# Pixels in natural order on ScalarE; the selection reads columns eight apart, the tail interleaves four quadrants into every second PSUM column

## The chip, the core and the metric

One NeuronCore of a Trainium2 chip. The metric is the device time of one execution in microseconds (us); lower is better.

## What is computed

The input is x, 16 images of 512 channels and 64 x 64 pixels in fp32. Two residual layers follow each other. The change lies in the first one.

```python
def spatial_descriptor(x, k):
    b, c, h, w = x.shape
    p = k // 2
    xp = jnp.pad(x, ((0, 0), (0, 0), (p, p), (p, p)))
    corrs = [jnp.sum(x * jax.lax.dynamic_slice(xp, (0, 0, di, dj), (b, c, h, w)), axis=1) for di in range(k) for dj in range(k)]
    return jnp.stack(corrs, axis=1)
...
gs = spatial_descriptor(x, k)                                # k = 5: 25 correlations with the neighbours
norm = jnp.sqrt(jnp.sum(gs * gs, axis=1, keepdims=True) + EPS)
gs = gs / norm
feat = jnp.concatenate([x, gs], axis=1)
out = jnp.einsum('bchw,oc->bohw', feat, W) + bias[None, :, None, None]
return jax.nn.relu(out)
...
x = x + _L0_conv_ref(_gn(x), L0_conv_W, L0_conv_bias)        # first layer, _gn is a group norm of 32 groups
x = x + _L1_conv_ref(_gn(x), L1_conv_w1, L1_conv_b1, L1_conv_w2, L1_conv_b2)   # max pools, chosen by channel
```

## The kernel before, in words

The first layer runs over 16 images, each in 8 chunks (`c`) of 8 rows, 512 pixels; so there are 128 chunks. The 512 channels lie on the partitions in four blocks (`ct`, and `o` for the output's four blocks). Every engine has its own written-out program, and semaphores alone tie them together. In the turn of chunk c each does this:

- **ScalarE (ACT)** squares and roots the descriptor's norm (lines 535 and 537), empties the four conv banks of chunk c-1 with a ReLU into `relu` (`conv_out`, line 520), and normalises chunk c+3: for each channel block one activation writes the fp32 value `g32` (line 506) and one its fp16 rounding `gh` (line 508). Between the second and the third block it copies the transposed blocks out of PSUM (`after`, line 528).
- **VectorE (DVE)** masks the Gram products (line 726), makes the reciprocal and the descriptor `fn` (745, 749), adds the ReLU to the residual (738) and takes its statistics (740), and forms the fp16 remainder `gl` = `g32` - `gh` (`low_parts`, line 713), beside the next image's input statistics (663).
- **TensorE (PE)**, in this order: `picks` (line 1101), a Gram block (line 1056), `norm` (1123), a Gram block, `tail` of chunk c-1 (1134), two Gram blocks, the convolution's first output block (1079 to 1081), `turn_blocks` (1114), the other three output blocks.
- **GpSimd and the SyncE queue** split the descriptor into fp16 parts and regroup it with twelve small DMAs into `tpair`.

A Gram block multiplies the pixels of two rows with those of four rows. Its product has a pixel of the pair on each partition and on each column; `band` keeps the columns within two pixels, and `bq` holds the masked blocks. `picks` then takes the 25 correlations out with one-hot matrices, one for each of four quadrants `t` of 32 output partitions; a matmul has only 32 output columns of the array, and a group of four works side by side. `tail` adds the descriptor's part of the convolution to the four conv banks, with the regrouped descriptor as moving operand.

For the picks, the pixel's column w = 8 j + k is split by its class k = 2 t + q. Before the change, the pixels of a row pair are stored sorted by class: `turned` and `classed` are views by which ScalarE reads x in steps of eight fp32 (32 bytes) and writes `gh` and `g32` without gaps, and by which it reads a conv bank without gaps and writes `relu` in steps of eight. The Gram blocks, the picks and the conv banks then all have class order, and each pick reads runs of eight neighbouring columns.

Before the Gram block that opens turn c+1's work, TensorE waits on `s_gl` for VectorE's remainder of chunk c+2, which was normalised in the turn before.

Of the kernel before, what the change touches and what calls it, by code (L numbers as in the profile page):

```python
# [16 lines left out]
C, H, W = 512, 64, 64  # L17
# [4 lines left out]
CW = ROWS * W  # L22
NB = H // 2
PAIRS = ROWS // 2
# [10 lines left out]
RING = 4  # L35
# [5 lines left out]
REP = 3 * 32  # L41
QUADS = 4
# [2 lines left out]

def const_arrays():


    p = np.arange(P)
    k, r, j = p // 16, p // 8 % 2, p % 8  # L50
    w = 8 * j + k
    band = (np.abs(w[:, None] - w[None, :]) <= KS // 2).astype(np.float32)


    pick = np.zeros((P, 3, 2, QUADS, 32), np.float32)
    for role in range(3):
        for e in range(2):
            for t in range(QUADS):
                di = r + 2 * (1 - role) - e
                rho = (k - 2 * t + 2) % 8  # L60
                ok = (np.abs(di) <= KS // 2) & (rho < 6)
                pick[p[ok], role, e, t, (rho * KS + di + 2)[ok]] = 1.0
    ssum = (p[:, None] // 32 == p[None, :] // 32).astype(np.float32) * 2.0 ** -12
    gavg = (p[:, None] // CG == p[None, :] // CG).astype(np.float32) / CG
    ident = np.eye(P, dtype=np.float32)
    before = (p[:, None] < p[None, :]).astype(np.float32)
    ones = np.ones((P, P), np.float32)
    return np.concatenate([band, pick.reshape(P, -1), ssum, gavg, ident, before, ones], axis=1)
# [18 lines left out]
def build(nc, x, wt, wturn, bias, w1t, b1, w2t, b2, consts, out):  # L87
    fp32, fp16, i32 = mybir.dt.float32, mybir.dt.float16, mybir.dt.int32
    ALU, ACT, AX = mybir.AluOpType, mybir.ActivationFunctionType, mybir.AxisListType
# [17 lines left out]
    with ctx:  # L107
# [3 lines left out]
        def sb(name, shape, dt):  # L111
            return ctx.enter_context(nc.sbuf_tensor(name, shape, dt))
# [3 lines left out]
        o = 0  # L116
# [8 lines left out]
        bias_sb = sb("bias_sb", [P, CT], fp32)  # L125
# [10 lines left out]
        gbias = sb("gbias", [P, CT], fp32)  # L136
# [7 lines left out]
        def take(n):  # L144
            pos[0] += n
            assert pos[0] <= ARENA
            return arena[:, pos[0] - n:pos[0]]

        take(2 * CT * PIX)
        gh = take(CT * RING * CW // 2).bitcast(fp16).rearrange("p (t n) -> p t n", t=CT)  # L150
        gl = take(CT * RING * CW // 2).bitcast(fp16).rearrange("p (t n) -> p t n", t=CT)
        g32 = take(2 * CW).rearrange("p (s n) -> p s n", s=2)
# [7 lines left out]
        tpair = take(CW).bitcast(fp16).rearrange("p (s n) -> p s n", s=2)  # L160
        relu = take(2 * CW).rearrange("p (s n) -> p s n", s=2)
# [64 lines left out]
        psum = ctx.enter_context(nc.psum_tensor("psum", [P, 8, 512], fp32))  # L226
# [70 lines left out]
        def xs(ct, lo, n, par):  # L297

            return arena[:, bass.ds(par * (CT * PIX) + (ct * PIX + lo), n)]

        def turned(a):

            return a.rearrange("p (u r j k) -> p u k r j", r=2, j=8, k=8)

        def classed(a):

            return a.rearrange("p (u k r j) -> p u k r j", k=8, r=2, j=8)

        def gram_parts(t):


            parts, row = [], 2 * t
            while row < min(2 * t + 4, H):
                end = min(2 * t + 4, H, (row // (RING * ROWS) + 1) * RING * ROWS)
                parts.append(((row - 2 * t) * W, (row % (RING * ROWS)) * W, (end - row) * W))
                row = end
            return parts
# [170 lines left out]
        def _(act):  # L488
# [5 lines left out]
            def normalise(i, c, first=False, between=None):  # L494

                n0 = (i * CH + c) * CT
                act.wait_ge(s_newton, 3 * i + 3)
                if not first:

                    act.wait_ge(s_chunk_used, i * CH + c - RING + 1)  # L500
                for ct in range(CT):
                    if not (isinstance(n0, int) and n0 + ct < 2):
                        act.wait_ge(s_gl, n0 + ct - 1)
                    act.sem_inc(s_carry_a, 1)
                    piece = turned(xs(ct, c * CW, CW, i % 2))
                    act.activation(classed(g32[:, ct % 2, :]), piece, ACT.Identity, bias=gbias[:, ct:ct + 1],  # L506
                                   scale=grstd[:, ct:ct + 1])
                    act.activation(classed(gh[:, ct, (c % RING) * CW:(c % RING + 1) * CW]), piece, ACT.Identity,  # L508
                                   bias=gbias[:, ct:ct + 1], scale=grstd[:, ct:ct + 1]).then_inc(s_gh, 1)
                    if between and ct == 1:  # L510
                        between()

            def conv_out(chunk, o):
                n = chunk * CT + o
                act.wait_ge(s_conv, n + 1)
                if isinstance(n, int) and n < 2:
                    pass
                else:
                    act.wait_ge(s_added, n - 1)
                act.activation(turned(relu[:, o % 2, :]), classed(psum[:, o, :]), ACT.Relu, bias=bias_sb[:, o:o + 1],  # L520
                               scale=1.0 / (SC * SC)).then_inc(s_relu, 1)

            def after(i, c):
# [6 lines left out]
            def image(i, last):  # L530
                for c in range(CH):
                    n = i * CH + c
                    first = isinstance(n, int) and n == 0
                    act.wait_ge(s_pick, n + 1)
                    act.activation(sq, psum[:, BANK_A, 0:QW], ACT.Square).then_inc(s_sq, 1)
                    act.wait_ge(s_norm, n + 1)
                    act.activation(sq, psum[:, BANK_N, 0:QW], ACT.Sqrt, bias=epsd[:, :]).then_inc(s_root, 1)
                    if not first:
                        for o in range(CT):
                            conv_out(n - 1, o)  # L540
                    if c + 1 < CH:
                        turn = lambda: after(i, c + 1)
                    elif not last:
                        turn = lambda: after(i + 1, 0)
                    else:
                        turn = lambda: None
                    if c + 3 < CH:
                        normalise(i, c + 3, first=first, between=turn)
                    elif not last:
                        normalise(i + 1, c + 3 - CH, between=turn)  # L550
                    else:
                        turn()
                    if c == STATS_AT and not last:
                        group_root(i + 1)
# [3 lines left out]
            for c in range(3):  # L558
                normalise(0, c, first=True)
# [494 lines left out]
        def _(pe):  # L1054
# [30 lines left out]
            def picks(i, c):  # L1085

                pe.wait_ge(s_after, i * CH + c + 1)
                if not (isinstance(i, int) and i == 0 and c == 0):
                    pe.wait_ge(s_fn, i * CH + c)
                half = (c % 2) * PAIRS * P  # L1090
                for e in range(2):
                    for k, role in enumerate((BEFORE, AFTER, SAME)):

                        u0 = 1 if role == BEFORE and c == 0 else 0
                        u1 = PAIRS - 1 if role == AFTER and c == CH - 1 else PAIRS
                        src = bq[:, role, half:half + PAIRS * P]\
                            .rearrange("p (u t q r j) -> p t r q u j", t=QUADS, q=2, r=2, j=8)
                        for t in range(QUADS):
                            dst = psum[32 * t:32 * t + 32, BANK_A, 0:QW]\
                                .rearrange("p (q u r j) -> p r q u j", q=2, r=2, j=8)  # L1100
                            last = pe.matmul(dst[:, e, :, u0:u1, :], pick[:, role, e, t, :], src[:, t, e, :, u0:u1, :],
                                             start=(e == 0 and k == 0), stop=True, skip_group_check=True)
                last.then_inc(s_pick, 1)
# [21 lines left out]
            def tail(i, c):  # L1125


                half = c % 2
                pe.wait_ge(grouped[half], (i * (CH // 2) + c // 2 + 1) * GROUPED)
                src = tpair[0:REP, half, :].rearrange("p (t q u s) -> p q u t s", t=QUADS, q=2, u=PAIRS)  # L1130
                for o in range(CT):
                    dst = psum[:, o, :].rearrange("p (u t q s) -> p q u t s", u=PAIRS, t=QUADS, q=2)
                    for par in range(2):
                        last = pe.matmul(dst[:, par], wd[0:REP, par * C + o * P:par * C + (o + 1) * P],  # L1134
                                         src[:, par], start=False, stop=True, skip_group_check=True)
                    last.then_inc(s_conv, 1)
# [148 lines left out]
```

## Time and profile before

| | |
|---|---|
| median of 3 runs | 4606.43 us (4600.07 to 4608.84) |
| the profiled execution | 4614.89 us, span of its core 4613.1 us |
| PE busy | 3847.0 us, 83% |
| DVE busy | 3520.3 us, 76% |
| ACT busy | 2589.7 us, 56% |
| first layer's loop, 128 chunks | from 81.67 us to about 2,610 us |
| mean granted TensorE clock | 0.928 of full speed |

Busy shares are means over two very different stages: the loop over the chunks, in which PE is busy nearly all the time, and the second layer, in which DVE is. A change in the first layer has to be read from the loop's turns: what ends the last wait of the engine that all others follow.

### The profile page before, as it was taken

How to read it: one execution, taken by the hardware profiler on the slowest of the kernel's cores; microseconds unless marked ns; L12 is line 12 of the kernel's file. 1: busy time of each engine (PE TensorE's matmuls, PEld its weight loads, DVE VectorE, ACT ScalarE, POOL GpSimd, SP SyncE). 2: the span in 40 equal slices, each digit the busy share in tenths (PEclk: the TensorE clock that was granted, in tenths of full speed). 3: DMA queues.
4: the chain of work that ended last, by engine and by line, in shares of the span. 5: the costliest groups of instructions: out<-in, count | busy, mean ns of one | idle time of the engine just before them, and what ended most of it. 6: DMA issues, size and time to landing. Idle time of an engine off the chain costs nothing. (4 is left out here: it accounts for less than half of the span.)

```text
span 4613.1 us, 73329 instructions
## 1 busy us (share of the span) xinstructions
PE 3847.0 (83%) x23656; PEld 2135.8 (46%) x23657; DVE 3520.3 (76%) x4010; ACT 2589.7 (56%) x2830; POOL 637.1 (14%) x624
## 2 busy tenths in 40 slices
PE   3999999999999999999989767898888777777665
PEld 2655555555555555555556443343333333323222
DVE  5676667667666765766665576899999999999994
ACT  4777777777777777777777434443333233232322
POOL 0000000000000000000000012333232322222221
PEclk9999999999999999999999878898899888888887
DMA  4233322323333232333321246553333333323221
GB/s 167 97 116 116 109 103 100 134 98 116 116 116 111 99 120 97 116 116 116 115 98 61 61 129 217 180 182 154 146 147 134 132 143 125 134 107 123 111 119 48
DMA packets 174313, 556.98 MB, mean 121 GB/s; under 512 B 91248, under 2 KB 91248, under 8 KB 157552
## 3 DMA queue, kind: packets, MB, share of 16 engines
q1 hardware_dynamic: 152016, 283.62, 17.7%
q0 software_dynamic: 21920, 268.59, 15.1%
q8 instruction: 206, 3.38, 0.3%
q14 instruction: 171, 1.40, 0.1%
HBM read 277.23 MB, written 274.86 MB: 120 GB/s over the span
## 5 line engine op out<-in xcount | busy, mean ns | idle before, releaser
L931 DVE TENSOR_TENSOR arena<-arena 128x2048 f32<-128x2048 f32 (+4 forms) x730 | 1759.1, 2430 | 107.7 <-ACT arena L579 66.3
L1250 PE MATMUL psum<-arena 128*128 128x512 f32 x1072 | 615.0, 658 | 442.0 <-issue 399.0
L1056 PE MATMUL psum<-arena 128*128 128x256 f16 (+1 forms) x6344 | 744.2, 272 | 152.7 <-DVE arena L713 134.8
L579 ACT ACTIVATE arena<-arena 128x4096 f32<-128x4096 f32 x67 | 244.2, 3645 | 972.3 <-DVE arena L931 706.6
L1079 PE MATMUL psum<-arena 128*128 128x512 f16 x2048 | 782.3, 382 | 0.7 <-ACT arena L520 0.7
L1080 PE MATMUL psum<-arena 128*128 128x512 f16 x2048 | 782.3, 382 | 0.0
L1081 PE MATMUL psum<-arena 128*128 128x512 f16 x2048 | 782.1, 382 | 0.0
L520 ACT ACTIVATE arena<-psum,bias_sb 128x512 f32<-128x512 f32 x512 | 577.5, 1184 | 270.6 <-PE psum L1134 171.3
L1056 PEld LDWEIGHTS psum<-arena 128*128 128x128 f16 x6344 | 597.4, 99 | 241.5 <-issue 124.1
L713 DVE TENSOR_TENSOR arena<-arena 128x512 f16<-128x512 f32 x512 | 351.7, 687 | 432.0 <-ACT arena L508 431.9
L506 ACT ACTIVATE arena<-arena,gbias,grstd 128x512 f32 (+1 forms) x512 | 669.3, 1307 | 6.0 <-DVE arena L713 4.7
L508 ACT ACTIVATE arena<-arena,gbias,grstd 128x512 f16 (+1 forms) x512 | 668.6, 1306 | 0.0
L1254 PE MATMUL psum<-arena 128*128 128x512 f32 x1072 | 579.9, 624 | 0.0
L1250 PEld LDWEIGHTS psum<-arena 128*128 128x128 f32 x1072 | 217.7, 210 | 738.3 <-issue 674.3
L599 ACT ACTIVATE arena<-psum,arena 128x512 f32<-128x512 f32 x536 | 336.0, 689 | 321.8 <-PE psum L1254 321.4
L1252 PE MATMUL psum<-arena 128*128 128x512 f32 x896 | 500.7, 642 | 0.0
L738 DVE TENSOR_TENSOR arena<-arena 128x512 f32 (+1 forms) x512 | 349.4, 682 | 141.8 <-ACT arena L520 141.8
L740 DVE BATCH_NORM_STATS2 bny<-arena 128x6 f32 (+1 forms) x512 | 355.4, 694 | 98.2 <-DVE arena L738 96.0
L409 POOL CAST arena<-arena 128x128 f16<-128x128 f32 x128 | 37.4, 292 | 2510.4 <-DVE arena L749 2510.4
L1254 PEld LDWEIGHTS psum<-arena 128*128 128x128 f32 x1072 | 219.2, 204 | 290.1 <-issue 290.1
L663 DVE BATCH_NORM_STATS2 bnx<-arena 128x6 f32 (+1 forms) x512 | 326.2, 681 | 11.3 <-DMA arena<-in_x 11.2
L1081 PEld LDWEIGHTS psum<-arena 128*128 128x128 f16 x2048 | 201.6, 98 | 245.5 <-issue 7.0
(138 smaller groups left out, 2672.0 us busy)
## 6 DMA issues: line engine op xcount, KB each, us to landing
arena<-in_x SPq DMA_DIRECT2D x64, 2048.0 KB, 12.6
y_planes<-arena SPq DMA_DIRECT2D x64, 2048.0 KB, 7.9
arena<-arena SPq DMA_DIRECT2D x1536, 8.0 KB, 1.7
arena<-plane_records,arena POOLq DMA_INDIRECT x67, 3.0
arena<-y_planes,arena POOLq DMA_INDIRECT x67, 9.4
out<-arena POOLq DMA_INDIRECT x67, 8.7
arena<-in_wt SPq DMA_DIRECT2D x1, 1024.0 KB, 12.6
cst<-in_consts SPq DMA_DIRECT2D x1, 768.0 KB, 4.3
```

The lines of the kernel that those rows point to most:

```text
L506: act.activation(classed(g32[:, ct % 2, :]), piece, ACT.Identity, bias=gbias[:, ct:ct + 1], scale=grstd[:, ct:ct + 1])
L508: act.activation(classed(gh[:, ct, (c % RING) * CW:(c % RING + 1) * CW]), piece, ACT.Identity, bias=gbias[:, ct:ct + 1], scale=grstd[:, ct ...
L520: act.activation(turned(relu[:, o % 2, :]), classed(psum[:, o, :]), ACT.Relu, bias=bias_sb[:, o:o + 1], scale=1.0 / (SC * SC)).then_inc(s_ ...
L740: dve.bn_stats(bny[:, o, c, :], y).then_inc(s_y, 1)
L931: ins = dve.tensor_tensor(dst, a, b, ALU.max)
L1056: return pe.matmul(dst, w, m, start=(k == 0), stop=(k == nk - 1))
L1079: pe.matmul(dst, h, gh[:, ct, slot], start=(ct == 0), stop=False)
L1080: pe.matmul(dst, h, gl[:, ct, slot], start=False, stop=False)
L1081: last = pe.matmul(dst, l, gh[:, ct, slot], start=False, stop=(ct == CT - 1))
L1250: pe.matmul(dst, diag[:, s, 0, :], bufs[:, u, b * CW:(b + 1) * CW], start=True, stop=False)
L1252: pe.matmul(dst, diag[:, s, 1, :], small[:, s, b * ROWS:(b + 1) * ROWS, 1:W + 1], start=False, stop=False)
L1254: pe.matmul(dst, diag[:, s, 2, :], big[:, s, b * CW:(b + 1) * CW], start=False, stop=True)\
```

## The change

ScalarE reads and writes natural pixel order everywhere. The class order moves into TensorE's access patterns: the picks read columns eight apart, and the tail's output goes to every second column of the conv bank. The constants that hold the order of the pixels on the partitions (`band`, `pick`) follow. No instruction is added, removed or moved: on each engine the sequence of instructions is the same, and only the shapes of the patterns differ.

```diff
     p = np.arange(P)
-    k, r, j = p // 16, p // 8 % 2, p % 8
-    w = 8 * j + k
+    r, w = p // W, p % W
+    k = w % 8
     band = (np.abs(w[:, None] - w[None, :]) <= KS // 2).astype(np.float32)
...
-        def turned(a):
-            return a.rearrange("p (u r j k) -> p u k r j", r=2, j=8, k=8)
-        def classed(a):
-            return a.rearrange("p (u k r j) -> p u k r j", k=8, r=2, j=8)
...
-                    piece = turned(xs(ct, c * CW, CW, i % 2))
-                    act.activation(classed(g32[:, ct % 2, :]), piece, ACT.Identity, bias=gbias[:, ct:ct + 1],
+                    piece = xs(ct, c * CW, CW, i % 2)
+                    act.activation(g32[:, ct % 2, :], piece, ACT.Identity, bias=gbias[:, ct:ct + 1],
                                    scale=grstd[:, ct:ct + 1])
-                    act.activation(classed(gh[:, ct, (c % RING) * CW:(c % RING + 1) * CW]), piece, ACT.Identity,
+                    act.activation(gh[:, ct, (c % RING) * CW:(c % RING + 1) * CW], piece, ACT.Identity,
                                    bias=gbias[:, ct:ct + 1], scale=grstd[:, ct:ct + 1]).then_inc(s_gh, 1)
...
-                act.activation(turned(relu[:, o % 2, :]), classed(psum[:, o, :]), ACT.Relu, bias=bias_sb[:, o:o + 1],
+                act.activation(relu[:, o % 2, :], psum[:, o, :], ACT.Relu, bias=bias_sb[:, o:o + 1],
                                scale=1.0 / (SC * SC)).then_inc(s_relu, 1)
...
                         src = bq[:, role, half:half + PAIRS * P]\
-                            .rearrange("p (u t q r j) -> p t r q u j", t=QUADS, q=2, r=2, j=8)
+                            .rearrange("p (u r j t q) -> p t r q u j", t=QUADS, q=2, r=2, j=8)
...
-                src = tpair[0:REP, half, :].rearrange("p (t q u s) -> p q u t s", t=QUADS, q=2, u=PAIRS)
+                src = tpair[0:REP, half, :].rearrange("p (t q s) -> p q s t", t=QUADS, q=2)
                 for o in range(CT):
-                    dst = psum[:, o, :].rearrange("p (u t q s) -> p q u t s", u=PAIRS, t=QUADS, q=2)
+                    dst = psum[:, o, :].rearrange("p (s t q) -> p q s t", t=QUADS, q=2)
```

A pick's 64 columns were eight runs of eight fp32; they are now 64 fp32 each 32 bytes from the one before. A tail matmul's 256 fp16 were sixteen runs of sixteen neighbours, and its output went to runs of 16 columns; now each fp16 lies 256 bytes from the one before (after every fourth it jumps back by three such steps, less one element), and the output goes to 256 columns, every second one of the bank.

## Rows read from the trace of the kernel before

**Rows 1.** The page's header, busy times and slices.

```profile
span 4613.1 us, 73329 instructions
PE 3847.0 (83%) x23656; PEld 2135.8 (46%) x23657; DVE 3520.3 (76%) x4010; ACT 2589.7 (56%) x2830; POOL 637.1 (14%) x624
...
PE   3999999999999999999989767898888777777665
...
DVE  5676667667666765766665576899999999999994
ACT  4777777777777777777777434443333233232322
```

**Rows 2.** Waits from 500 to 2500 us: total us, times, longest.

```profile
ACT arena L520 <- PE psum L1134: 130.1, 99, 2.5
...
PE psum L1056 <- DVE arena L713: 99.1, 63, 1.9
...
PE psum L1142 <- ACT arena L528: 21.4, 12, 1.8
...
PE psum L1114 <- DVE arena L732: 4.8, 22, 0.3
```

**Rows 3.** PE in order of time: start, length, idle time before in brackets.

```profile
1555.20 0.38 PE L1081 MATMUL psum<-arena 128*128 128x512 f16 x1
1555.51 0.88 PE L1101 MATMUL psum<-arena,cst 128*32 128x64 f32 x48
1557.81 1.48 PE L1056 MATMUL psum<-arena 128*128 128x256 f16 x12 [1.42 <-DVE arena L713]
1559.12 0.39 PE L1123 MATMUL psum<-arena,cst 128*128 128x128 f32 x2
1559.35 1.47 PE L1056 MATMUL psum<-arena 128*128 128x256 f16 x12
1560.66 1.04 PE L1134 MATMUL psum<-arena 96*128 96x256 f16 x8
1561.53 2.81 PE L1056 MATMUL psum<-arena 128*128 128x256 f16 x36
```

**Rows 4.** ACT in order of time, the end of the same turn.

```profile
1554.43 1.31 ACT L506 ACTIVATE arena<-arena,gbias,grstd 128x512 f32 x1
1555.65 1.30 ACT L508 ACTIVATE arena<-arena,gbias,grstd 128x512 f16 x1
1556.86 0.25 ACT L535 ACTIVATE arena<-psum 128x128 f32<-128x128 f32 x1
```

**Rows 5.** Groups by form from 500 to 2500 us: count, busy us, mean ns.

```profile
L1123 PEld LDWEIGHTS psum<-arena,cst 128*128 128x128 f32 x200 | 31.8, 201 | 1.5
L506 ACT ACTIVATE arena<-arena,gbias,grstd 128x512 f32 x396 | 517.9, 1308 | 4.1 <-DVE arena L713 4.1
...
L520 ACT ACTIVATE arena<-psum,bias_sb 128x512 f32<-128x512 f32 x398 | 450.1, 1183 | 212.5 <-PE psum L1134 130.1 <-DVE arena L738 72.6
...
L528 ACT ACTIVATE arena<-psum 128x512 f32<-128x512 f32 x87 | 50.5, 580 | 0.0
...
L528 ACT ACTIVATE arena<-psum 128x384 f32<-128x384 f32 x13 | 6.1, 470 | 0.0
```

**Rows 6.** The same of the whole run: contiguous activation with a bias pointer.

```profile
L599 ACT ACTIVATE arena<-psum,arena 128x512 f32<-128x512 f32 x536 | 336.0, 689 | 321.8 <-PE psum L1254 321.4
```

**Rows 7.** Start of the run in order of time: first normalisation, first Gram block, later waits.

```profile
45.21 1.30 ACT L506 ACTIVATE arena<-arena,gbias,grstd 128x512 f32<-128x512 f32 x1 [1.33 <-DVE gbias L703]
...
55.66 4.15 PE L1056 MATMUL psum<-arena 128*128 128x256 f16 x24 [13.42 <-DVE arena L713]
...
74.05 0.69 DVE L713 TENSOR_TENSOR arena<-arena 128x512 f16<-128x512 f32 x1 [1.70 <-ACT arena L508]
...
75.22 4.58 PE L1056 MATMUL psum<-arena 128*128 128x256 f16 x24 [15.42 <-DVE arena L726]
```

**Rows 8.** DVE in order of time, one turn: first mask, first residual, last remainder.

```profile
1539.79 0.42 DVE L726 TENSOR_TENSOR arena<-psum,cst 128x256 f32<-128x256 f32 x1 [0.46 <-PE psum L1056]
...
1543.19 0.69 DVE L738 TENSOR_TENSOR arena<-arena 128x512 f32 x1 [1.07 <-ACT arena L520]
...
1549.85 0.67 DVE L713 TENSOR_TENSOR arena<-arena 128x512 f16<-128x512 f32 x1
...
1554.56 0.69 DVE L713 TENSOR_TENSOR arena<-arena 128x512 f16<-128x512 f32 x1 [0.99 <-ACT arena L508]
1555.17 1.28 DVE L663 BATCH_NORM_STATS2 bnx<-arena 128x6 f32 x2
1556.98 0.69 DVE L713 TENSOR_TENSOR arena<-arena 128x512 f16<-128x512 f32 x1 [0.53 <-ACT arena L508]
```

## The prediction

> **What bounds the kernel now.** I read the page's slices first. The run has two stages: up to slice 22 or 23 PE is in the nines while DVE and ACT have room, after that DVE is in the nines [rows 1]. The change touches nothing in the second stage, so the question is the length of a turn in the first. The norm's matmul shows two weight loads per turn, and 200 of them in 2,000 us give 100 turns of 20.0 us [rows 5].
>
> The waits come next. PE waits for DVE's remainder (L713) 99.1 us in those 100 turns, for ACT's copy (L528) 21.4 us, and 4.8 us for a mask [rows 2]: 125 us, 1.25 us a turn. Read against time, this is one chain. PE has finished its convolution and the picks by 1556.4 and starts the next Gram block at 1557.81 [rows 3]; the last remainder runs from 1556.98 [rows 8], and it waits for the last normalisation, which ACT starts at 1555.65 and ends at 1556.95 [rows 4]. So ACT, though it has idle time earlier in the turn (it waits 130.1 us for the tail's banks [rows 2]), delivers last and costs PE over a microsecond. The rest of the turn, 18.75 us, is PE's own work and sequencer pauses. The reader is to see that PE is nearly full and that ACT's lateness is the only large thing that a cheaper ACT can return.
>
> **What ACT gives back.** Twelve activations per turn lose their 32-byte steps. Now a normalisation takes 1308 ns and a ReLU 1183 [rows 5]. The nearest row without steps is the second stage's activation of 512 columns with a bias pointer, 689 ns [rows 6], so each gets about 0.6 us (normalisation) or 0.5 us (ReLU) shorter: 8 x 0.62 + 4 x 0.49 = 6.9 us per turn. ACT then has its normalisations done several microseconds before PE asks, and the waits for L713 and L528 go in full: -1.25 x 128 = -160 us. What is late next if nothing else changed is DVE: from its first mask (1539.79) to the start of the last remainder (1556.98) lie 17.2 us, with 0.99 and 0.53 of waits for ACT in it, and 1.07 for the first ReLU, which comes 0.5 earlier [rows 8]. Without these 2.0 us, and with the remainder itself (0.7 us) and the Gram block ahead of the first mask (1.3 us), the loop over DVE is some 17.2 us, under PE's 18.75. So PE's own work is the bound, and DVE's slack covers the gain.
>
> At the start PE waits 13.42 and then 15.42 us while ACT normalises three chunks alone; from 45.21 to the last remainder at 74.05 these are 24 activations of 1.2 us each from start to start [rows 7]. At 0.6 us each this is 24 x 0.6 = 14 us shorter. Sum of gains: 174 us.
>
> **What TensorE pays.** PE's work is on the path everywhere, so each nanosecond added to it counts 128 times.
>
> The tail: eight matmuls of 256 fp16 columns occupy 1561.53 - 1560.66 = 0.87 us, 109 ns each, 0.43 ns a column [rows 3]. The picks: 48 records in groups of four side by side are 12 steps in 0.88 us less the 0.22 that the last one takes to end, 55 ns for 64 columns, 0.87 ns a column [rows 3]. No row of PE shows a moving operand in which every column is a hop, nor an output to every second column. The bounds:
> - Below: no cost, as a run of 16 or of 8 neighbours reads at full rate.
> - Above, by the nearest row: ScalarE reads the same SBUF in the same 32-byte hops. Its normalisation costs (1308 - 689) / 512 = 1.2 ns a column more than the row without hops [rows 5, 6]; that row's slope is (580 - 470) / 128 = 0.86 ns a column [rows 5], so a hop costs about 2.0 ns. The ReLU, which only writes in hops, gives nearly the same.
> - Between: PE reads fp32 at 0.87 ns a word; if a hop takes two such slots, it is 1.74 ns.
>
> I take the middle of the last two, 1.87 ns a hopping column, because two independent streams on ScalarE (read and write) both show a price near 2 ns that belongs to the memory rather than to the engine, and because fp16 gives PE nothing to combine when neighbours are 256 bytes apart. Tail: 256 x 1.87 = 479 ns instead of 109, 8 x 0.370 = +2.96 us. Picks: 64 x 1.87 = 120 ns instead of 55 per step, 12 x 0.064 = +0.77 us. Together +3.73 us a turn, x 128 = +477 us.
>
> The Trainium skill (Advanced Engine Details and Errata, "Memory Cachelines") says that SBUF has 16-byte lines, that two hits on a line are needed to hide its latency, and that in PSUM any non-contiguous pattern significantly slows a matmul, pairs of neighbours being wanted. This speaks against both edited patterns; it gives no figure, and the trace agrees with its SBUF half on ScalarE (1308 against 689 ns), while no row shows the PSUM half.
>
> DVE's loop grows by less: the first ReLU comes after two tail matmuls, 0.74 us later, and 17.9 us stays under the turn of 22.5 that PE then has.
>
> **The sum.** On the profiled execution: 4614.9 - 174 + 477 = 4918. The profiled time stands 8.5 us over the median of the runs, so 4909 us. With 1.74 ns a hop the tail adds 2.69 and the picks 0.67 us, +430 us: 4862. With 2.0 ns, 3.22 + 0.87 = 4.09 us, +524 us: 4956. This likeliest case spans 4860 to 4960.
>
> **The rivals.**
> - The tail only doubles. If PE fetches each hop in one 0.83 ns slot of its word stream (or if only the output to every second column counts, two columns' time for one), a tail matmul takes 213 ns, +0.83 us a turn. With the picks dear (+0.77) this is 1.60 x 128 = +205 us: 4629. With the picks free it is +107 us: 4539. For it: PE's interface feeds fp16 at twice ScalarE's element rate, and the picks' four side-by-side streams show that it sustains more than one read at once [rows 3]. Against: ScalarE's price of a hop [rows 5].
> - TensorE doesn't mind hops at all, and the change does what ACT's rows promise: 4614.9 - 174 - 8.5 = 4432. For it: runs of 16 fp16 with jumps between already cost nothing, 109 ns for 256 columns like the Gram blocks (1.47 us for 12 and a tail end) [rows 3]. Against: ScalarE's reading, which is also free of any arithmetic reason to be slow.
> - Hops dearer than on ScalarE, as four pick streams start at nearly the same addresses and the tail's hops of 256 bytes may meet the same part of the memory: at 2.5 ns the tail adds 4.25, the picks 1.25 us, +704 us: 5137.
>
> The sign turns where PE's addition reaches 174 / 128 = 1.36 us a turn. With one price s for all 2048 tail and 768 pick columns, 2816 s = 0.87 + 0.67 + 1.36, s = 1.03 ns a column: under that the change is faster.
>
> **How the numbers follow.** Likeliest case 0.48; tail doubled with dear picks 0.15; tail doubled with free picks 0.13; free 0.11; dearer 0.13. The likeliest case's own range is 4860 to 4960; the range for 8 in 10 takes in both doubled cases below and a third of the dearer one above: 4530 to 5000. A measurement of this kernel tells 0.2% (9 us) from no change. Slower is the likeliest case, the dearer one and most of the first doubled case (0.11): 0.72; faster is free, doubled with free picks and a little of the other: 0.25; same 0.03.
>
> **What would show it.** Right: L506 and L508 near 690 ns, ReLU near 690; no wait of PE for L713 or L528 beyond a microsecond in all; tail matmuls starting over 400 ns apart, the picks' burst about 1.6 us, the turn 22.5 us, ACT idle waiting for the tail. Wrong on the price: tail matmuls 109 or 213 ns apart. Wrong on the gain: PE still waiting for L713 with DVE busy just before, or the Gram blocks and convolution slower though their patterns are as before.

## The result: 4.8% slower, and the profile after

The median of four runs is 4821.71 us (4818.33 to 4829.57) against 4603.25 us (4597.22 to 4608.84) before; the ratio is 1.0477, with a 95% interval of 1.0456 to 1.0498. The profiled execution has a span of 4823.3 us.

The page's header and busy times after. In kernels made from the change the line numbers are nine lower than before: L1056 is now L1047, L1101 L1092, L1134 L1125, L713 L704, L506 L497, L520 L511.

```profile
span 4823.3 us, 73329 instructions
PE 4235.3 (88%) x23656; PEld 2230.7 (46%) x23657; DVE 3528.9 (73%) x4010; ACT 1891.0 (39%) x2830; POOL 646.1 (13%) x624
```

ACT has lost 699 us of work and PE has gained 388; DVE's is the same [rows 1]. The next fence is the busy time by stretch, first of before, then of after, each from the first pick of the first turn to the first pick of the last, 127 turns. The columns are stretch and length, then PE, PEld, DVE, ACT and POOL busy with counts, granted clock, DMA share and GB/s.

```profile
81.70:2608.80 2527.10, 2335.72 (x20294) 1467.05 (x20294) 1670.14 (x3083) 1897.79 (x1900) 91.35 (x254) 0.99 0.30 105
```

```profile
69.80:2817.40 2747.60, 2722.82 (x20294) 1563.88 (x20294) 1678.52 (x3083) 1216.13 (x1900) 90.97 (x254) 0.99 0.27 97
```

The reader is to see three things. The loop starts 11.9 us earlier. A turn takes 2747.6 / 127 = 21.63 us where it took 19.90, 220.5 us more in the loop; 220.5 - 11.9 is 209 of the 210 us by which the two spans differ, so the second stage took no part. And PE's idle time is 24.8 us, 0.20 us a turn, where it was 191.4, 1.51 us a turn: the gain that was promised did come, and PE's own work grew by 387 us over it.

TensorE in order of time after, the counterpart of [rows 3]:

```profile
1602.74 1.49 PE L1092 MATMUL psum<-arena,cst 128*32 128x64 f32 x48
1604.16 1.48 PE L1047 MATMUL psum<-arena 128*128 128x256 f16 x12
1605.48 0.39 PE L1114 MATMUL psum<-arena,cst 128*128 128x128 f32 x2
1605.70 1.47 PE L1047 MATMUL psum<-arena 128*128 128x256 f16 x12
1607.02 3.64 PE L1125 MATMUL psum<-arena 96*128 96x256 f16 x8
1610.48 1.71 PE L1047 MATMUL psum<-arena 128*128 128x256 f16 x14
```

No bracket stands behind any row: nothing waits. Eight tail matmuls take 1610.48 - 1607.02 = 3.46 us, so they start 433 ns apart instead of 109; that is 1.7 ns a column. The picks are a burst of 1.49 us instead of 0.88. The Gram blocks, whose patterns the change leaves alone, keep their 1.48 us. The groups by form from 500 to 2500 us, and one row of the waits there:

```profile
L1125 PE MATMUL psum<-arena 96*128 96x256 f16 x736 | 335.3, 612 | 0.0
L497 ACT ACTIVATE arena<-arena,gbias,grstd 128x512 f32 x368 | 296.7, 806 | 129.3 <-DVE arena L704 129.3
...
L511 ACT ACTIVATE arena<-psum,bias_sb 128x512 f32<-128x512 f32 x368 | 252.9, 687 | 452.2 <-DVE arena L729 258.7 <-PE psum L1125 193.5
```

```profile
ACT arena L526 <- PE psum L1092: 357.1, 92, 7.0
```

A normalisation takes 806 ns (1308 before) and a ReLU 687 (1183) [rows 5]. PE's waits for DVE's remainder and for ACT's copy, 99.1 and 21.4 us in [rows 2], have left the list; now ACT waits for PE's picks.

### The profile page after: what moved, and what is told of

Its sections match the earlier page's. It is cut to its first block and busy times, and to the rows that moved or that the text cites. A ratio compares the mean times of both kernels' runs of the same rounds, so it can differ in the third digit from the quotient of the medians.

```text
span 4823.3 us, 73329 instructions
## 1 busy us (share of the span) xinstructions
PE 4235.3 (88%) x23656; PEld 2230.7 (46%) x23657; DVE 3528.9 (73%) x4010; ACT 1891.0 (39%) x2830; POOL 646.1 (13%) x624
## 5 line engine op out<-in xcount | busy, mean ns | idle before, releaser
L1047 PE MATMUL psum<-arena 128*128 128x256 f16 (+1 forms) x6344 | 750.3, 273 | 18.4 <-DVE arena L704 9.5
L1047 PEld LDWEIGHTS psum<-arena 128*128 128x128 f16 x6344 | 604.5, 100 | 195.8 <-issue 107.3
L717 DVE TENSOR_TENSOR arena<-psum,cst 128x256 f32<-128x256 f32 x448 | 187.7, 419 | 599.8 <-PE psum L1047 599.8
L511 ACT ACTIVATE arena<-psum,bias_sb 128x512 f32<-128x512 f32 x512 | 351.8, 687 | 632.6 <-DVE arena L729 353.9
L497 ACT ACTIVATE arena<-arena,gbias,grstd 128x512 f32 (+1 forms) x512 | 412.7, 806 | 166.7 <-DVE arena L704 165.4
L1125 PE MATMUL psum<-arena 96*128 96x256 f16 x1024 | 466.4, 612 | 0.0
L704 DVE TENSOR_TENSOR arena<-arena 128x512 f16<-128x512 f32 x512 | 343.4, 681 | 134.5 <-ACT arena L499 134.5
L499 ACT ACTIVATE arena<-arena,gbias,grstd 128x512 f16 (+1 forms) x512 | 409.7, 800 | 0.0
```

What stands on the lines that cost most here:

```text
L497: act.activation(g32[:, ct % 2, :], piece, ACT.Identity, bias=gbias[:, ct:ct + 1], scale=grstd[:, ct:ct + 1])
L499: act.activation(gh[:, ct, (c % RING) * CW:(c % RING + 1) * CW], piece, ACT.Identity, bias=gbias[:, ct:ct + 1], scale=grstd[:, ct:ct + 1]) ...
L1047: return pe.matmul(dst, w, m, start=(k == 0), stop=(k == nk - 1))
```

## The experiments

The theory after the result has two parts. The gain is the removal of PE's waits for ACT. The loss is PE's own, and within it a price of reading SBUF: a read brings up to 8 neighbouring bytes in a slot of about 1.7 ns, so a hop at every element wastes half of a slot with fp32 and three quarters with fp16. The main rival for the loss is the tail's output to single PSUM columns, which the change brought in at the same place; a rival for the whole is that ACT's and PE's parts interact. Time differences are against the change's 4822 us where nothing else is said. Where only one run was made, the time is that run's.

### ScalarE's half alone

```diff
-                            .rearrange("p (u r j t q) -> p t r q u j", t=QUADS, q=2, r=2, j=8)
+                            .rearrange("p (u t q r j) -> p t r q u j", t=QUADS, q=2, r=2, j=8)
...
-                src = tpair[0:REP, half, :].rearrange("p (t q s) -> p q s t", t=QUADS, q=2)
+                src = tpair[0:REP, half, :].rearrange("p (t q u s) -> p q u t s", t=QUADS, q=2, u=PAIRS)
...
-                    dst = psum[:, o, :].rearrange("p (s t q) -> p q s t", t=QUADS, q=2)
+                    dst = psum[:, o, :].rearrange("p (u t q s) -> p q u t s", u=PAIRS, t=QUADS, q=2)
```

> ScalarE in natural order as after the change, picks and tail with the access patterns of before, so the picks select and the tail places the wrong pixels; the amount of work is the same. It measures the gain alone. Theory (PE's waits for ScalarE go in full, PE's own work stays): 4603 - 1.25 x 128 - 12 at the start = 4431 us, a turn of 18.4 to 18.8 us, tail matmuls 109 ns apart. Rival (DVE's loop comes next and eats part of it): 4450 to 4550 us, with PE waiting for L713's successor and DVE busy just before.

Measured: 4407.5 us, ratio to before 0.9554 (0.9538 to 0.9570). The stretch of 127 turns, columns as above:

```profile
69.60:2410.40 2340.80, 2296.11 (x20294) 1463.03 (x20294) 1657.74 (x3083) 1202.19 (x1900) 94.44 (x254) 1.00 0.32 114
```

That is 18.43 us a turn, 1.47 less than before, and PE is idle for 0.35 us of it. ScalarE's half is worth 4.5%; its time is 24 us under the 4431 expected. Beside pauses of PE's sequencer, one wait of PE is left from 500 to 2300 us:

```profile
PE psum L1047 <- DVE arena L704: 10.2, 12, 0.9
```

DVE's loop thus takes back 0.1 us a turn. PE's idle time fell by 1.51 - 0.35 = 1.16 us a turn. The other 0.31 us is PE's busy time, which for the same matmuls is 2296.1 us where it was 2335.7. Part of that goes with the granted clock. Of the 85 slices of 20 us from 600 to 2300 us, 17 had a clock of 0.96 or less before, nearly all 0.91, and 4 have it here; 13 slices fewer at 20 x 0.09 = 1.8 us are an estimated 23 us.

### TensorE's half alone

The kernel before, with the constants, the picks and the tail of the change and ScalarE's `turned` and `classed` kept, so that its lines have the numbers of before.

> The other part of the change alone: picks and tail with the new patterns, ScalarE as before in its hops, so the picks and the tail take wrong pixels. The amount of work is the same. Theory (TensorE's work is the bound once it is longer, and ScalarE's lateness hides behind it): tail 435 ns, a turn of 21.7 to 21.9 us, 4822 + 12 for the slow start, 4834 to 4860 us; TensorE's waits for VectorE near zero. Rival (the tail lies on ScalarE's own loop, whose delay adds to it): 20.05 + 3.24 = 23.3 us a turn, 5020 us, with the waits of before.

Measured: 4862.84 us, ratio to before 1.0559 (1.0540 to 1.0579). The waits from 500 to 2500 us:

```profile
DVE arena L713 <- ACT arena L508: 288.4, 217, 2.2
...
PE psum L1142 <- ACT arena L528: 8.7, 12, 0.7
...
PE psum L1056 <- DVE arena L713: 5.1, 14, 0.4
```

DVE still waits for ACT, but PE hardly for DVE: 5.1 us where it was 99.1 [rows 2]. The halves don't add. ScalarE's is worth about 200 us alone and some 40 us beside TensorE's; TensorE's costs 255 us alone and 414 us beside ScalarE's (4822 - 4407.5). A turn's length is what the busier chain needs, and (414 - 255) / 127 = 1.25 us a turn of PE's new work fell into its old waits. PE's idle time says nearly the same: 54.1 us in 127 turns (83.8 to 2861.5 us), 0.43 us a turn, where it was 1.51. Of the 40 us over the change some 11 lie in the later start and the rest in the loop. The time came out 3 us above the expected range.

### Which side of the tail pays

The first kernel walks the tail's columns by quadrant, so its read has runs of 64 and its output steps of eight columns. The second keeps the hopping read and writes neighbours; it adds to the wrong pixels.

```diff
-                src = tpair[0:REP, half, :].rearrange("p (t q s) -> p q s t", t=QUADS, q=2)
+                src = tpair[0:REP, half, :].rearrange("p (t q s) -> p q t s", t=QUADS, q=2)
...
-                    dst = psum[:, o, :].rearrange("p (s t q) -> p q s t", t=QUADS, q=2)
+                    dst = psum[:, o, :].rearrange("p (s t q) -> p q t s", t=QUADS, q=2)
```

```diff
-                    dst = psum[:, o, :].rearrange("p (s t q) -> p q s t", t=QUADS, q=2)
+                    dst = psum[:, o, :].rearrange("p (q s t) -> p q s t", t=QUADS, q=2)
```

> After the change, but each tail matmul walks its 256 columns by quadrant: the moving fp16 are read in four runs of 64 neighbours, and the output goes to every eighth PSUM column. Same result. Theory R (the tail pays for the hops of its SBUF read, 435 instead of 109 ns): back to 109 ns, 4822 - 8 x 0.326 x 128 = 4488 us. Rival W (it pays for writing single PSUM columns): the tail stays at 435 ns and the time at 4822 us; if single PSUM columns cost two slots, 213 ns and 4594 us.

> After the change, with the tail's hopping read as it is, but its output in one run of 256 neighbouring PSUM columns for each half, so it adds to the wrong pixels. Theory R: no change, tail matmuls 435 ns apart, 4822 us. Rival W: 109 ns apart, 4488 us.

Runs read: 4592.22 us, ratio to before 0.9961 (0.9946 to 0.9975). TensorE in order of time in that kernel:

```profile
1622.91 1.89 PE L1125 MATMUL psum<-arena 96*128 96x256 f16 x8
1624.60 1.57 PE L1047 MATMUL psum<-arena 128*128 128x256 f16 x13
```

Eight matmuls in 1.69 us, 211 ns apart (216 after the first), not 109. Runs written: the group by form there is

```profile
L1125 PE MATMUL psum<-arena 96*128 96x256 f16 x715 | 325.7, 611 | 0.0
```

611 ns as after the change, where the rival wanted the 273 of before. The first kernel's time is the rival's, which gave 4594 us for a price of two slots on the output; the second kernel has no gain at all, and that speaks for the read. So neither theory had it whole: with the hopping read the output's pattern makes no difference, but once the read is mended the output to single columns sets a second limit, at about twice the full rate's time. The dearer of the two decides, they do not add. The 4898.14 us of the second kernel were above what both theories gave; that is taken up below.

### Pairs in the picks

The columns of a pick are walked with q innermost, so that two neighbouring fp32 are read between hops, and written 64 PSUM columns apart in turn.

```diff
-                            .rearrange("p (u r j t q) -> p t r q u j", t=QUADS, q=2, r=2, j=8)
+                            .rearrange("p (u r j t q) -> p t r u j q", t=QUADS, q=2, r=2, j=8)
...
-                                .rearrange("p (q u r j) -> p r q u j", q=2, r=2, j=8)
+                                .rearrange("p (q u r j) -> p r u j q", q=2, r=2, j=8)
```

> After the change, but each pick walks its 64 columns as 32 pairs of neighbouring fp32 (both q of a quadrant), each pair 32 bytes from the one before, and writes them to PSUM columns 64 apart in turn. Same result. Theory G (what costs is a read of 8 bytes per slot, so pairs run at full rate): the picks' step goes from 118 back to 55 ns, 4822 - 12 x 0.055 x 128 = 4737 us. Rival L (each new 16-byte line costs, however many words are taken from it, or the alternating PSUM columns cost): the step stays at 90 to 118 ns, 4790 to 4822 us.

Measured: 4743.59 us, ratio to before 1.0280 (1.0263 to 1.0297), 78 us under the change. A record of the picks from 500 to 2500 us:

```profile
L1092 PE MATMUL psum<-arena,cst 128*32 128x64 f32 x4176 | 85.4, 223 | 28.4 <-issue 28.4
```

223 ns is the value of before; after the change it was 297. Pairs of fp32 cost next to nothing, though each pair is on a new place 32 bytes on: a whole burst of 48 is 0.90 us long at 1603.77 us, where it was 0.88 [rows 3]. The outputs that alternate between far columns are in this time too; a pick takes 55 / 64 = 0.87 ns a column anyway.

### The same pairs on ScalarE

```diff
-            return a.rearrange("p (u r j k) -> p u k r j", r=2, j=8, k=8)
+            return a.rearrange("p (s t q) -> p t s q", t=4, q=2)
...
-            return a.rearrange("p (u k r j) -> p u k r j", k=8, r=2, j=8)
+            return a.rearrange("p (t s q) -> p t s q", t=4, q=2)
```

> The kernel before, but ScalarE walks pairs of neighbouring fp32 (8 bytes), each 32 bytes from the one before, where it walked single fp32; what it stores is then in another order than the picks and the tail take it to be, so they take wrong pixels. The amount of work is the same. Theory G (8 bytes of a read or write per slot, so pairs are free): normalisations near 806 ns and ReLUs near 687 as in e1_scalar_only, 4408 us. Rival L (a new 16-byte line costs, however much is taken from it): normalisations 1050 to 1300 ns, and 4500 to 4603 us.

Measured: 4406.56 us, as ScalarE's half alone. The lines have the numbers of before. Two groups by form from 500 to 2300 us:

```profile
L506 ACT ACTIVATE arena<-arena,gbias,grstd 128x512 f32 x386 | 326.9, 847 | 115.2 <-DVE arena L713 114.7 <-issue 0.5
...
L520 ACT ACTIVATE arena<-psum,bias_sb 128x512 f32<-128x512 f32 x388 | 270.0, 724 | 286.0 <-DVE arena L738 158.7 <-PE psum L1134 127.3
```

847 ns when ACT reads pairs and 724 when it writes them, against 1308 and 1183 with single words [rows 5]: both directions want 8 neighbouring bytes, and some 40 ns remain.

### How many bytes a slot brings

The tail's output goes to neighbours (and adds to the wrong pixels), so that only the read counts, and the read takes runs of four or two fp16 between its hops of 256 bytes.

```diff
-                src = tpair[0:REP, half, :].rearrange("p (t q s) -> p q s t", t=QUADS, q=2)
+                src = tpair[0:REP, half, :].rearrange("p (t q a s) -> p q a t s", t=QUADS, q=2, s=4)
...
-                    dst = psum[:, o, :].rearrange("p (s t q) -> p q s t", t=QUADS, q=2)
+                    dst = psum[:, o, :].rearrange("p (q a t s) -> p q a t s", t=QUADS, q=2, s=4)
```

For runs of two, `s=2` stands in both lines.

> As e3_tail_runs_write (the tail adds to the wrong pixels, its output goes to neighbouring PSUM columns), but its read takes runs of four neighbouring fp16 (8 bytes) between hops of 256 bytes. Theory G (each slot of about 1.7 ns brings up to 8 bytes): tail matmuls 109 ns apart, a turn of 21.70 - 2.59 = 19.1 us, 4822 - 334 = 4488 us. Rival L (a slot brings one 4-byte word of a new place): 217 ns and 4600 us, or dearer.

> As e9_runs_of_four with runs of two fp16 (4 bytes). Theory G: half of 8 bytes used in each slot of 1.70 ns, tail matmuls 217 ns apart, 4822 - 8 x 0.218 x 128 = 4599 us. Rival (the cost is one of odd half words, so full 4-byte words are free): 109 ns, 4488 us.

The groups by form from 500 to 2300 us, runs of four first:

```profile
L1125 PE MATMUL psum<-arena 96*128 96x256 f16 x752 | 99.6, 273 | 0.0
```

```profile
L1125 PE MATMUL psum<-arena 96*128 96x256 f16 x720 | 174.3, 398 | 0.0
```

One burst of each, up to the next Gram block, runs of four first:

```profile
1602.84 1.06 PE L1125 MATMUL psum<-arena 96*128 96x256 f16 x8
1603.74 2.78 PE L1047 MATMUL psum<-arena 128*128 128x256 f16 x24
```

```profile
1604.04 1.94 PE L1125 MATMUL psum<-arena 96*128 96x256 f16 x8
1605.80 2.80 PE L1047 MATMUL psum<-arena 128*128 128x256 f16 x24
```

Eight matmuls take 0.90 us with runs of four, 112 ns each and so 3% over the 109 of before, and 1.76 us with runs of two, 220 ns. The times are 4494.82 and 4599.69 us; theory G gave 4488 and 4599. For each new place that is 433 / 256 = 1.69, 220 / 128 = 1.72 and 112 / 64 = 1.75 ns, whether 2, 4 or 8 bytes come from it. Whether more than 8 bytes could come in that time isn't shown: at full rate TensorE takes just 8 (four fp16 at 0.43 ns, two fp32 at 0.87), so a fixed 1.7 ns for each new place, hidden once 8 bytes are taken from it, tells the same story. All pairs and runs of four here start on a multiple of 8 bytes within their tile; others weren't tried.

### Both mends together, and the output's distance

> After the change, with both mends together: the tail's read in runs of 64 with its output to every eighth PSUM column, and the picks in pairs. Same result. Theory (costs of TensorE add, since it never waits): tail matmuls 216 ns apart, picks' steps 55 ns, a turn of 19.90 - 0.65 = 19.25 us, 4592 - 83 = 4509 us, 2% under the kernel before. Rival (once TensorE is shorter, VectorE's loop or ScalarE ends the turn): 4530 to 4590 us with TensorE waiting before the Gram block.

> As e5_runs_and_pairs, but the tail's output goes to every second PSUM column as in the change instead of every eighth, so it adds to the wrong pixels; its read is in runs of 64. Theory W2 (a lone fp32 word written in PSUM costs two slots at whatever distance): tail matmuls 216 ns apart, 4509 us. Rival (a small step stays cheap, so that the change's own output pattern was free and e2_tail_runs_read created the 216 ns itself): 109 ns, 4509 - 8 x 0.107 x 128 = 4399 us.

The first is the change with the two walks above, the tail by quadrant and the picks in pairs. The second has the same walks, and its output goes by `"p (t s q) -> p q t s"`, to the wrong pixels. The first measured 4512.69 us (4504.03 to 4518.51), ratio to before 0.9796 (0.9783 to 0.9809). TensorE in order of time, the tail of one turn:

```profile
1611.26 1.89 PE L1125 MATMUL psum<-arena 96*128 96x256 f16 x8
1612.95 2.83 PE L1047 MATMUL psum<-arena 128*128 128x256 f16 x24
```

It beats both kernels, but it is 105 us over ScalarE's half alone, and 8 x (211 - 109) ns x 128 = 104 us, worked out from the spacings, are the price of the tail's lone output columns. They can't be paired by another walk: the two neighbours q go through different weights, `par` in `tail`, and so through different matmuls. The second, whose tail adds to every second column, as in the change, takes 4504.83 us. Its group by form from 500 to 2500 us:

```profile
L1125 PE MATMUL psum<-arena 96*128 96x256 f16 x832 | 196.8, 416 | 0.0
```

416 ns is the mean of the kernel with steps of eight as well, against 273 before. A lone column costs the same at a distance of two or of eight, so the change's own output pattern carried this price, hidden under its read.

### The run that was too slow

> e3_tail_runs_write once more, timed. Its one run took 4898 us with the tail at 435 ns as after the change; the granted clock was 0.96 between 1600 and 2600 us where after the change it was 0.99. If that dip belongs to the pattern: 4890 to 4900 us again, clock 0.96. If it was that execution's alone: 4815 to 4830 us, clock 0.98 to 0.99.

Measured: 4905.37 us (4902.35 to 4910.24), ratio to before 1.0651 (1.0619 to 1.0682), so the first run's time was no accident of that execution; it is 5 us above what was expected if the dip belongs to the pattern. The stretch from 600 to 2300 us, of the change and then of this kernel:

```profile
600.00:2300.00 1700.00, 1683.00 (x12544) 965.51 (x12546) 1059.25 (x1949) 760.10 (x1186) 55.87 (x156) 0.99 0.29 104
```

```profile
600.00:2300.00 1700.00, 1682.60 (x12217) 963.02 (x12218) 1040.53 (x1903) 742.63 (x1154) 55.15 (x154) 0.97 0.28 100
```

PE is busy for the same share, but gets through 12217 matmuls instead of 12544, 2.6% fewer, at a granted clock of 0.97 instead of 0.99. The 127 turns, from the first `norm` to the last, take 2818.0 us instead of 2747.0. Two hundredths of the loop's 2,750 us are about 55 of these 71 us; 2.6% would be 72. The surplus is thus mostly the granted clock, and no price of the write. Three slices of 20 us show how it falls, first of the change, then of this kernel:

```profile
1500.00:1520.00 20.00, 20.00 (x159) 11.13 (x158) 14.87 (x26) 9.36 (x14) 0.72 (x2) 1.00 0.30 112
1520.00:1540.00 20.00, 20.00 (x137) 11.15 (x139) 15.46 (x27) 9.46 (x14) 0.72 (x2) 1.00 0.03 6
1540.00:1560.00 20.00, 20.00 (x134) 11.46 (x127) 12.15 (x27) 9.62 (x15) 0.71 (x2) 1.00 0.28 100
```

```profile
1500.00:1520.00 20.00, 20.00 (x153) 12.13 (x152) 15.21 (x31) 7.67 (x12) 0.00 (x0) 0.93 0.57 208
1520.00:1540.00 20.00, 20.00 (x138) 10.84 (x137) 13.54 (x23) 9.47 (x14) 0.72 (x2) 0.91 0.33 117
1540.00:1560.00 20.00, 20.00 (x149) 11.29 (x150) 15.32 (x27) 9.45 (x14) 0.72 (x2) 1.00 0.30 111
```

Within the second of them one microsecond shows the lower of the clock's two levels, 1.2 GHz:

```profile
1524.00:1525.00 1.00, 1.00 (x7) 0.69 (x5) 0.29 (x1) 0.00 (x0) 0.00 (x0) 0.50 0.10 17
```

PE was busy without a pause, the slow tail included. The change's clock falls too, only less often. Of the 85 slices from 600 to 2300 us, 7 have 0.96 or less in the change, 33 in this kernel and 33 in its first run. The contiguous write alone doesn't do it: with the same output and the read in runs of four or two it is 11 and 4. So the clock falls more often where the contiguous write stands beside the single-fp16 read. Why is open. The tail reads the same data in the same order as in the change, but its sums land on other pixels, and no run here separates the two.

## Why the prediction was right, and where its sizes were off

The direction, the mechanism and the wide range of 4530 to 5000 us held. The forecast of 4909 us was 87 us too high, and the likeliest case's own range of 4860 to 4960 us missed the measured 4822. The two errors, too little gain and too much cost, point the same way, so no luck of one cancelling the other is in the result. By its own steps:

- *What bounds the kernel.* PE's waits for ACT's late normalisation are what a cheaper ACT gives back, and nearly all of it came: ScalarE's half alone is 0.9554 of before. The sum had 174 us of gain; the experiment shows 204 (4612.04 - 4407.5, on its own chip). In the change's trace the start gave 11.9 us where 14 were summed. With ScalarE's half alone the loop gave 1.47 us a turn where 1.25 were summed. Of this 1.16 us is idle time, a little under the sum, and 0.31 us is PE's shorter busy time, which the sum didn't have and of which by the estimate above over half goes with the granted clock.
- *What ACT gets back.* 806 ns for a normalisation, not 689: the row taken as nearest [rows 6] reads PSUM, this one SBUF and with its scale from a pointer too; which of the two takes the 117 ns wasn't tried. It cost nothing, since ACT is not the bound.
- *What TensorE pays, tail.* Taken at 1.87 ns a column, measured at 1.70, 433 ns a matmul instead of 479: 8 x 0.046 x 128 = 47 us of the error. This is the largest mis-sized term. The lower end of the likeliest case, twice the 0.87 ns of an fp32 word, was the right reading: 1.74 gives 4862, and with the gain at 204 it gives 4832.
- *What TensorE pays, picks.* +0.77 us a turn was summed. The burst grew from 0.88 to 1.49 us, +0.61 in the turn shown, and mending the picks alone gave 78 us back, 0.61 us a turn. That is 0.16 us less, 20 us of the error.
- *ScalarE's price of a hop stands for TensorE's.* It does to within a sixth, and the experiments show the same measure on both: pairs of fp32 take away nearly all of the price. On ScalarE a hop costs more, (1308 - 806) / 512 = 1.0 ns over the full rate of 0.86, 1.8 ns in all, nearer still to TensorE's 1.7 than the 2.0 that I had from the PSUM row. The prediction called the ReLU's price nearly the same; its own rows gave (1183 - 689) / 512 + 0.86 = 1.82 ns, which would have put the middle of the likeliest case at 1.78 instead of 1.87.
- *The rival with a doubled tail* was wrong for the change but right as a second limit: 211 ns a matmul is what the output to lone PSUM columns costs once the read is mended. Its 4629 us with dear picks is a slip: 4614.9 - 174 + 205 - 8.5 is 4637. The range doesn't hang on it.

The Trainium skill's rule (Advanced Engine Details and Errata, "Memory Cachelines") that two consecutive PSUM elements should be contiguous is borne out by the 211 ns. The Trainium skill's two hits on an SBUF line (the same section) are not the measure: two neighbouring fp16 still cost 220 ns, four cost 112, and a burst of picks that reads pairs of fp32 takes 0.90 us where it took 0.88. The Trainium skill (Vector Engine (DVE) Microarchitecture Reference, "Measured stream behaviour on trn2") states for VectorE that pairs of neighbouring 4-byte words, starting on an 8-byte boundary, run at the full rate whatever the hop between them. Here TensorE behaves so (223 ns a pick in pairs and before), and ScalarE to within 5% (847 against 806 ns).

## What to carry to other kernels

An order that has to change somewhere costs least where the engine has time, but first look whether the same elements can be walked so that each hop brings 8 neighbouring bytes: then the read costs next to nothing on either engine, and here a loss of 4.8% became a gain of 2%, with the tail's lone output columns still paid for. A matmul has a read pattern and a write pattern, and the dearer one decides; mending one shows the other. And price a pattern change on TensorE by columns times slot, since on a full engine nothing hides it, while the gain on the engine that was only late ends where its lateness ends.

## What the runs showed of the hardware

- A moving operand of TensorE costs about 1.7 ns for each new place, from which 8 neighbouring bytes come without more time: fp16 in runs of one, two and four take 433, 220 and 112 ns for 256 columns, 109 at full rate. ScalarE reads and writes SBUF by nearly the same measure (1308 ns with single fp32, 847 with pairs, 806 without hops; 1183, 724 and 687 for the write).
- A matmul whose fp32 output goes to lone PSUM columns takes 211 ns for 256 columns, at steps of two and of eight alike. An fp32 matmul of 0.87 ns a column shows no such price when its output alternates between columns 64 apart.
- With the single-fp16 read, a contiguous write instead of a stepped one moved the granted clock of a loop from 0.99 to 0.97 and 0.96 in two profiled runs with PE equally busy; with the read in longer runs it stayed at 0.99 and 1.00.
